# First attention of a four-layer kernel: gate features stacked into 96 rows, product with the values waiting per quarter, norm moved ahead of the probabilities

## What is computed

```python
emb = box_relational_embedding(boxes)            # sines and cosines of 100*log of box distances, 16 per pair
g = relu(einsum('bnmd,hd->bhnm', emb, Wg) + bg)  # one gate per head and pair of rows
q = (queries @ Wq.T + bq); k = (keys @ Wk.T + bk); v = (values @ Wv.T + bv)   # 16 heads of 64
a = einsum('bhqd,bhkd->bhqk', q, k) / sqrt(64)
mn = softmax(log(clip(g, 1e-6)) + a, axis=-1)    # computed as max(g, 1e-6) * exp(a), normalised
out = einsum('bhqk,bhkd->bqhd', mn, v) @ Wo.T + bo
```

## Time and profile before

| | |
|---|---|
| median of 3 runs | 1144.31 us (1140.92 to 1145.85) |
| profiled execution | 1143.62 us, span of its trace 1141.6 us |
| busy share: PE, weight loads, DVE, ACT, POOL | 83%, 68%, 72%, 60%, 62% |
| mean granted TensorE clock | 0.929 of 2.4 GHz |
| first attention, steady part | batches 2 to 14, 23.6 to 23.7 us each, within 100 to 410 us |
| its end | from 410 us to about 471 us |

### The profile page before, as it was taken

One profiled execution on the slowest core, in us unless ns is written; L12 is line 12 of the kernel. 1 busy time (PEld: TensorE's weight loads), 2 busy tenths in 40 slices (PEclk: granted clock), 3 DMA queues, 4 the chain that ended last, 5 costly groups with the idle time before them and its releaser, 6 DMA issues.

```text
span 1141.6 us, 32938 instructions
## 1 busy us (share of the span) xinstructions
PE 949.0 (83%) x12178; PEld 777.1 (68%) x12178; DVE 817.9 (72%) x1957; ACT 684.2 (60%) x1342; POOL 710.1 (62%) x811
## 2 busy tenths in 40 slices
PE   0448999999999985589876569982899999999995
PEld 0336777777777764455544458861899999999995
DVE  3997888788877876677877689956566666666663
ACT  2457888888888883066543468854354454545452
POOL 2988888875777653035453279965466666666662
PEclk9889999999999997689988789985899999999998
DMA  9277776787767656411000100003553225832251
GB/s 280 76 188 150 135 150 153 157 175 171 146 154 159 137 109 167 143 51 41 1 1 1 40 2 21 21 21 100 165 152 103 33 40 168 268 91 32 32 143 14
DMA packets 52117, 119.65 MB, mean 105 GB/s; under 512 B 7616, under 2 KB 30144, under 8 KB 51632
## 3 DMA queue, kind: packets, MB, share of 16 engines
q0 software_dynamic: 14144, 35.48, 21.6%
q1 hardware_dynamic: 35520, 80.71, 21.1%
q10 hardware_dynamic: 2352, 2.10, 0.6%
HBM read 212.54 MB, written 37.85 MB: 219 GB/s over the span
## 4 chain that ended last, share of the span: by engine, by line
PE 53%; DVE 14%; POOL 11%; ACT 9%; DMA 7%; issue 5%; SPq 0%; ACTq 0%; POOLq 0%; DVEq 0%
PE bank L2168 17%; PE bank L2182 8%; POOL PT L565 6%; PE bank L1827 5%; PE bank L1730 3%; PE bank L1929 3%; DVE nmx L1209 2%; PE bank L1968 2%; PE bank L1807 2%; ACT EX L1424 2%; PE bank L1941 2%; PE bank L1769 2%; ACT L1393 1%; PE bank L1762 1%; DMA gates<-in_g_ffn 1%
## 5 line engine op out<-in xcount | busy, mean ns | idle before, releaser
L1664 ACT ACTIVATE yg<-bank,bms 128x128 f32<-128x128 f32 x312 | 106.9, 363 | 113.2 <-PE bank L2168 103.3
L1327 DVE TENSOR_TENSOR hm<-hf,hm 128x256 f16<-128x256 f32 x156 | 66.7, 427 | 90.8 <-ACT hm L1671 87.0
L1322 DVE SCALAR_TENSOR_TENSOR hf<-bank,bms,yg 128x128 f32<-128x128 f32 x312 | 98.8, 347 | 32.1 <-ACT yg L1664 29.4
L2168 PE MATMUL bank<-xT,wm_even 128*128 128x128 f16 x1920 | 116.2, 221 | 1.9 <-DVE xT L1334 1.0
L709 POOL DMA_INDIRECT out_x<-ys,sidx x39 | 62.7, 1608 | 83.2 <-DVE ys L1341 83.2
L2168 PEld LDWEIGHTS bank<-xT,wm_even 128*128 128x128 f16 x1920 | 111.5, 99 | 3.5 <-DVE xT L1334 1.4
L2168 PE MATMUL bank<-xT,wm_odd 128*128 128x128 f16 x1824 | 109.9, 220 | 2.0 <-DMA wm_odd<-expert_weights 2.0
L2168 PEld LDWEIGHTS bank<-xT,wm_odd 128*128 128x128 f16 x1824 | 105.5, 99 | 3.1 <-issue 2.2
L1671 ACT ACTIVATE hm<-hf 128x256 f16<-128x256 f32 x156 | 64.7, 415 | 63.9 <-DVE hf L1322 62.8
L565 POOL TENSOR_TENSOR PT<-PT 128x512 f16<-128x512 f32 x64 | 72.3, 1157 | 41.7 <-ACT PT L1450 41.6
L551 POOL TENSOR_TENSOR q<-qt,q 128x512 f16<-128x512 f32 x64 | 79.9, 1276 | 1.0 <-ACT q L1437 0.9
(11 more groups left out here) (309 smaller groups left out, 2660.2 us busy)
## 6 DMA issues: line engine op xcount, KB each, us to landing
wm_even<-expert_weights SPq DMA_DIRECT2D x60, 1024.0 KB
wm_odd<-expert_weights SPq DMA_DIRECT2D x57, 1024.0 KB
expert_weights<-in_wcat POOLq DMA_DIRECT2D x16, 768.0 KB, 7.8
wsp<-expert_weights SPq DMA_DIRECT2D x16, 768.0 KB, 4.4
wsp<-in_wcat POOLq DMA_DIRECT2D x16, 768.0 KB, 10.6
expert_weights<-wsp SPq DMA_DIRECT2D x16, 768.0 KB, 3.3
Lst<-gate_tables SPq DMA_DIRECT2D x48, 68.0 KB, 5.8
gate_tables<-Lw SPq DMA_DIRECT2D x6, 512.0 KB, 4.6
```

What stands on the lines that cost most here:

```text
L1322: v.scalar_tensor_tensor(hf[:, (c // 2) % 2, c % 2, :], bank[c % 4][:, MT:2 * MT], bms[:, par, FC + c:FC + c + 1], yg[:, c % 4, :], ALU.ad ...
L1327: v.tensor_tensor(hm16[:, par, 1, c - 1:c + 1, :], hf[:, q % 2, :, :], hm16[:, par, 0, c - 1:c + 1, :], ALU.subtract).then_inc(m_hl, 1)
L1664: s.activation(yg[:, c % 4, :], bank[c % 4][:, 0:MT], ACT.Gelu, bias=bms[:, par, c:c + 1]).then_inc(m_g, 1)
L2168: ins = t.matmul(bank[c % 4][:, w * MT:(w + 1) * MT], wm16[par][:, wp, col:col + P], xT16[:, par, xp * KD + kk, :], start=(n == 0), stop=( ...
```

## The change

Gate features: `Fst` is a new tile of 96 rows in four planes, one for each group of four keys: rows 0 to 31 and 32 to 63 the high part of the features, rows 64 to 95 the low part. SP fills it from `F16s` by 12 transfers a batch, 8 of the high part and 4 of the low part, each of 32 rows and 1,024 columns (64 KB). `We16` becomes 96 rows (high, low, high) by 64 columns (16 heads by 4 keys), so that one matmul of 96 rows and 64 columns takes the place of three parts for four keys: a quarter has eight such instead of six of 256 columns. `F16s` and `Fst` have one buffer each; the writers of `F16s` wait for the stacking transfers of the batch before (`s_fst`), and PE waits for those of its own batch.

Product with values: the wait for the low part of the probabilities is taken per quarter. Norm: batch b+3 is normed ahead of `probs(b)`, instead of b+2 at the start of the next iteration. `bn_stats` moves between the halves of `take_qk`. The semaphore between the two operations of `residual` is replaced. On SP `store_tables(1)` moves from batch 8 to the end of batch 7.

```diff
-        F16s = sb("F16s", [P, 2, 2, NJ * N], F16, l0)
+        F16s = sb("F16s", [P, 2, NJ * N], F16, l0)
+        Fst = sb("Fst", [P, NN // QN, NJ * N], F16, l0)
...
+            def stack_high(b):
+
+                sp.wait_ge(s_fhi, b + 1)
+                if b:
+                    sp.wait_ge(s_gf, 4 * b)
+                for q in range(NN // QN):
+                    for k in range(2):
+                        sp.dma_start(Fst[k * QR:k * QR + QR, q, :], F16s[q * QR:q * QR + QR, 0, :]).then_inc(s_fst, 16)
+
+            def stack_low(b):
+
+                sp.wait_ge(s_flo, b + 1)
+                for q in range(NN // QN):
+                    sp.dma_start(Fst[2 * QR:3 * QR, q, :], F16s[q * QR:q * QR + QR, 1, :]).then_inc(s_fst, 16)
+
             for par in range(2):
                 next_ctx(par, par)
+            stack_high(0)
             store_tables(0)
             for par in range(2):
                 load_tables(par)
+            stack_low(0)
             for par in range(2):
                 load_half(0, par, True)
-            for i in range(1, B // 2 - 1):
-                for par in range(2):
-                    next_ctx(i * 2 + par, par)
-                    if i * 2 + par == NJ:
-                        store_tables(1)
-                    load_tables(i * 2 + par)
-                    store_half(i - 1, par)
-                    load_half(i, par)
-            for par in range(2):
-                load_tables(B - 2 + par)
-                store_half(E - 2, par)
-                load_half(E - 1, par)
-
+            for b in range(2, B):
+                par = b % 2
+                if b < B - 2:
+                    next_ctx(b, par)
+                load_tables(b)
+                stack_high(b - 1)
+                stack_low(b - 1)
+                store_half(b // 2 - 1, par)
+                load_half(b // 2, par)
+                if b == NJ - 1:
+                    store_tables(1)
+
+            stack_high(B - 1)
+            stack_low(B - 1)
             store_half(E - 1, 0)
...
             def feature_low(n, par):
                 gp.wait_ge(s_fhi, n + 1)
-                nc.gpsimd.tensor_tensor(F16s[:, par, 1, :], fs, F16s[:, par, 0, :], ALU.subtract).then_inc(s_flo, 1)
+                if n:
+                    gp.wait_ge(s_fst, STK * n)
+                nc.gpsimd.tensor_tensor(F16s[:, 1, :], fs, F16s[:, 0, :], ALU.subtract).then_inc(s_flo, 1)
...
             def iteration(b, par, has_c, has_q, has_x, first=False):
-                if has_x:
+                if not has_c:
                     norm(b + 2, b + 2)
                 row_max(b, (0, 1))
                 if has_q:
                     take_qk(b + 1, (0, 1))
+                if b > 1:
+                    v.bn_stats(bst[:, b - 2, :], X[:, b - 2, :])
                 row_max(b, (2, 3))
...
                     feature_distance(b + 2, par)
+                if b + 3 < B:
+                    norm(b + 3, b + 3)
                 probs(b, not has_c)
-                if has_c:
-                    v.bn_stats(bst[:, bass.ds(b - 1, 1), :].rearrange("p o c -> p (o c)"), X[:, bass.ds(b - 1, 1), :].rearrange("p o d -> p (o d)"))
...
-                s.activation(F16s[:, par, 0, :], fs, ACT.Copy).then_inc(s_fhi, 1)
+                if n:
+                    ac.wait_ge(s_fst, STK * n)
+                s.activation(F16s[:, 0, :], fs, ACT.Copy).then_inc(s_fhi, 1)
...
             def gate(b, par, g, first, has_q):
                 if g == 0:
-                    pe.wait_ge(s_flo, b + 1)
+                    pe.wait_ge(s_fst, STK * (b + 1))
...
-                    for n, (wp, fp) in enumerate(PAIRS):
-                        ins = t.matmul(bk[:, jj * 256:(jj + 1) * 256], F16s[:, par, fp, j * N:(j + 1) * N], We16[:, wp, :], start=False,
-                                       stop=(n == 2), skip_group_check=True)
+                    part = bk[:, jj * 256:(jj + 1) * 256].rearrange("p (h q i) -> p q h i", h=H, q=NN // QN)
+                    for q in range(NN // QN):
+                        ins = t.matmul(part[:, q, :, :], Fst[0:FR, q, j * N:(j + 1) * N], We16[0:FR, :], start=False, stop=True,
+                                       skip_group_check=True)
                 ins.then_inc(s_gf, 1)
 
             def pv(c, par, first):
-                pe.wait_ge(s_pl, 4 * c + 4)
                 pe.wait_ge(s_vl, 2 * c + 2)
                 for f in range(4):
+                    pe.wait_ge(s_pl, 4 * c + f + 1)
```

52 lines of the change are left out of this document (28 added, 24 removed).

## The result

The changed kernel takes 1164.41 us (median of 4 runs, 1161.54 to 1168.19) beside 1144.55 for the kernel before: a ratio of 1.0181, 95% interval 1.014 to 1.0222. It is slower by about 20 us. The forecast was 1142.3 with a range from 1132 to 1152, so the measured time lies 12 us above its upper end. The profiled execution took 1162.43 us with a span of 1160.4, 18.8 us more than before.

What follows compares the result with a forecast made beforehand. PE was taken to bound only from the product with values to the output projection, with DVE close behind. Loop -9.9, batch 8 +4.4, end +4.25, start 0: -1.25 us on 1143.6 gives 1142.3, range 1132 to 1152.

Steps and rivals of the forecast that it cites:

- Gate matmuls: PE's gates: eight 64-column matmuls take 0.30 us a quarter, saving 0.53 a quarter, 2.1 a batch, mostly becoming PE idle time.
- Rival D: PE's gates: eight weight loads at 97 ns fill a quarter's 0.8 us, so periods stay unchanged; 1149.6 us, chance 0.08.
- Values per quarter: Product with values: its first quarter starts when the k projection ends, removing DVE's 0.23 us wait (1.06 in first batch).
- From there to the output projection the chain is the same: After DVE's divisions: the product's end moves with DVE, not POOL, with the chain to the output projection as before.
- Norm and bn_stats: DVE: same work in other places; delays `PT` by about 0.35 us, covered; possible 2.6 us loop gain taken as 0.
- Stacking transfers in a normal batch: SP's 12 transfers into `Fst`: 0.42 us per issue, 7.0 us of room for landing, no cost.
- rival C: Every batch: the stack lands late, PE stands 1.2 us in each of 14 batches; 1159 us, chance 0.12.
- Batch 8 on SP: Batch 7's stacking queues behind the second tables' stores and loads on SP: costs 4.4 us once, bounds 3.2 and 9.3.
- End of the attention: Last stacking issues delay SP's loads of the next layer's weights, for which DVE waits: costs 4.25 us, bounds 3.5 and 6.
- Start: First stacking pushes table stores and loads 3.4 us back, but PE idles behind the first gate: costs 0, at most 1.
- A: SP's single waits cost little because SP is ahead or other work hides them; 1133.7 us, chance 0.12.
- B: PE bounds the period after all, so the gates' 2.1 us come off each period; 1123 us, chance 0.07.

## Why the prediction was wrong, step by step

- **"Gate matmuls", 0.30 us a quarter.** Measured 0.41 us for eight (0.83 before). A second quarter starts 0.66 us after the first, before 1.08. Rival D's 0.8 us did not happen, and PE's busy time in a period fell from 22.33 to 20.8 us. The direction was right, the size 0.11 off.
- **"Values per quarter" and DVE's 0.62 + 0.23.** Right as to the waits: gone. Wrong as to what they were worth, and this is the step that failed: "What PE and POOL can give back per batch before DVE holds the chain is 0.62 + 0.23 = 0.85 us". The loop's gain was 0 (1.1 us in one batch), not 9.9. I took the idle time of DVE as the slack of the chain. The chain between DVE's last division and `project_o` ran through the floor and ACT's Ln, and the floor was tied to POOL's next operation already in the kernel before. The profile said so: the floor ended 0.54 to 0.56 us after POOL's first split in 14 batches. With that tie undone the change brings 0.94 us a batch from batch 8 on (0.88 beside the kernel before with the same order of POOL's work), near the 0.85 forecast.
- **"From there to the output projection the chain is the same."** That sentence left out POOL. My text had named the mechanism, for `norm`, with the page of the Trainium skill, and did not apply it to the other operation next to POOL's.
- **"Norm and bn_stats".** The norm fell from 0.84 to 0.41 us in the early batches; that was worth nothing by itself, since the floor stood for POOL there as well.
- **"Stacking transfers in a normal batch", 0.** Right: no waits of PE for `Fst` in ordinary batches, rival C did not occur. The issue price was wrong, 0.59 us in the median and 0.72 for a row of eight beside other traffic, not 0.42.
- **"Batch 8 on SP", 4.4 us (3.2 to 9.3).** Right in kind and place, mis-sized: 12.1. Of the difference, issue was 7.9 us (255.32 to 263.26) instead of 5.0, landing 6.8 instead of 3.3 (the row of `Lst` had said 5.8 in the median and 8.2 at most; I took the store of a half instead, with the reason that the accumulating transfer had just ended, and did not look at POOL's next copy, issued at 249.49 in the kernel before and ahead of the stacking's end in the changed one), and about 2 us came from PE's clock after the stall, which I had not put in at all.
- **"End of the attention", 4.25.** Measured 4.5; right.
- **"Start", 0 to 1.** Measured 6.1, and the loads of the tables began 8.6 us later (69.77 before, 78.37 now) instead of 3.4. I followed the first gate, which is not what counts there. Behind the tables on SP's queue stands `load_half(0)`, and ACT's negation of it precedes the exponentials. The step failed in "the first gate has idle time of PE behind it until the exponentials": the exponentials moved too. 4.5 of the 6.1 us went with the stores put first again.

Of the signs I had named, the unchanged period came true, but not for rival D's reason. A and B are out as well: the single waits cost 22.7 us, and the 2.1 us a batch that PE saved in its gates did not come off the period. Sum of what happened: 0 for the loop (but 1.1 in the one batch), 6.1 + 12.1 + 4.5, about 21.5 us to the end of the attention; the forecast had -9.9 + 0 + 4.4 + 4.25.

## What to carry to other kernels

An idle gap is not the slack of the chain if the next operation behind it can stand inside its own duration: before counting on a gap, compare each duration with the shortest one of the same line, and look whether its end keeps a fixed distance to another engine's. When work is added to an in-order queue, follow every transfer queued behind it to its last reader, also in the first and the last pass; price issues by how many stand in a row, and landings by the nearest row with the same target and traffic. A stall of TensorE costs more than its length.

## What the hardware showed that I had not expected

- A wait of DVE for POOL is booked as duration, not as idle time: the floor 0.68 us alone and up to 1.69 us beside POOL.
- It can outlast one operation of POOL. A 0.34 us operation stood up to 4.1 us through several operations of POOL in a row, and an update of X of 0.48 us took 1.83, from inside POOL's second split of v until 0.29 us behind the end of the split of the context that followed it. The Trainium skill (SBUF — State Buffer, Who interferes with whom) speaks of a block for the whole instruction of the one that was first. Here it was several instructions in two cases and one in the third, and the short operation stood although it had started 0.73 us ahead of POOL's first split; the measurement stands. What was ahead of it was POOL's DMA issue, by 0.07 us. Whether that issue hands what it holds to the splits behind it, and why POOL let the floor in after one operation and not the short ones, no run here shows.
- Issuing 64 KB transfers from one partition range of SBUF to another took SP 0.51 to 1.80 us each, 0.59 in the median; eight in a row 5.0 us, and up to 7.5 beside 1.5 MB of table stores.
- The landing of the last such transfer of batches 7 and 8 took 2.0 to 3.7 us where it was issued ahead of POOL's copy of a half expert, and 5.0 to 8.4 us where it was issued behind it.
- After a stall of PE of 10.24 us its granted clock was 0.50 for 7.1 us more, and 0.69 for the next 4.0.
